# State update of a chunked scan as three half-precision products, with the decay spread moved to ScalarE

## Chip, cores and metric

One core of one Trainium2 chip runs the whole program in one launch. The metric is device microseconds from start to end of that launch.

## The reference, cut to what matters

The program is four layers, each an attention-like part and a feed-forward part. The change is in the attention part of layer 2, which is a selective state space scan. Cut to its core, with 64 heads of 64 channels, 128 state rows and 8 groups of 8 heads:

```python
proj = hidden @ in_proj_w.T           # gate, x, B, C, dt
xBC = silu(causal_conv(proj, 4 taps)) # x, B, C
dA, dtx = exp(dt_p * A), dt_p * x
state = state * dA_t + dtx_t * B_t    # one step per token, for each head
y_t = state @ C_t
out = (rmsnorm(y + x * D) * silu(gate)) @ out_proj_w.T
```

## The kernel before, in words

The scan is done in chunks of 128 tokens. There are 16 chunks of tokens (two sequences of eight) and 8 groups of heads, so the part makes 128 turns: an outer loop over groups `gi` (the first and the last written out, the six between in a hardware loop), and inside it `x` from 0 to 3 and `c` from 0 to 3, turn `j = 4x + c`. Below, "turn 12" is j = 12 of a group, and a "c=2 turn" is any of turns 2, 6, 10, 14.

Each engine has its order written out by hand, as a function `slot(gi, x, c)`, and the engines meet at semaphores.

**PE** in turn j: `chunk(j)` (L2482: the product of the old state with C, L2487; the products inside the chunk, eight heads, L2495; the state update, L2499), `along(j+1)` (L2460: eight 128x128 products, L2467, that carry the decay along the tokens), a tile of the input projection for the next four turns (`in_proj`, 12 matmuls of 128x512 f16 through the helper `three`, L257 to L259), `to_tokens(j+1)` (L2471: transposes, L2478 and L2480, that wait for the state on VectorE by `m4_sk`), a second tile, `out_proj(j-1)` (L2501: the sum of squares, L2507, then 12 matmuls), `between(j+2)` (L2449, L2456) and `b_dot_c(j+2)` (L2439, L2447). Only in c=0 and c=1 turns a third tile of the projection stands between `b_dot_c(j+2)` and `chunk(j+1)`. In c=2 and c=3 turns `chunk(j+1)` follows at once.

**VectorE** in turn j: `from_state` (L2225), `mask` (L2201), `state(j)` (L2228: L2237 scales the state in SBUF, L2238 adds PSUM), `outputs` (L2245, L2248), `stepped(j+1)` (L2210, two L2217: token inputs times the step, f32 into `m4_x12`), the taps of the convolution (L2181), `variance(j-1)` (L2254), `masked(j+1)` (L2208), more taps, and `add_out(j-1)` (L2257, L2266), which waits for the root from GpSimd (`m4_rk`). The pieces of the next weights (L1869) are made in turns 0, 1 and 10 to 13, the parameters of the next group (L2162, L2163) at the start of turn 12.

**ScalarE** in turn j: evictions of projection tiles (`before`, L2001 and L2002; `gate`, L2009), `step_decay(j+1)` (L2032, waits for `along`), `b_tokens(j+1)` (L2039), `skipped(j+1)` (L2047), `square(j)` (L2054), the nonlinearity of the convolution (L2018), `gated(j)` (L2060, waits for PE's `out_proj(j-1)`), and `decays(j+2)` (two L2026, behind a load of the table for Exp). Pieces of the weights are L1855 and L1858.

**GpSimd** in turn j: `spread(j+2)` (L2275: two L2282, 128x1024 f16, and two L2287, 128x512 f16, the heads' decays spread over channels into `m4_ab`, for `along`), the gating product (L2307), two sums of squares (L2309, waits for `square`; L2311), the low plane of the output (L2314), and `root(j-1)` (L2292, L2296).

A semaphore count stands behind each of these; a buffer is single unless said, so `m4_ab` is written again only when `along` has read it.

## Time and profile before

| | us |
|---|---|
| median of 3 runs | 4071.8 (4069.22 to 4078.91) |
| the profiled execution's own time | 4070.89 |
| span of its instructions | 4069.1 |
| first L2487 to last L2499 of the scan, on PE | 1478.8 to 3400.7 |
| PE busy | 3592.1 |
| VectorE busy | 2897.5 |
| ScalarE busy | 2361.3 |
| GpSimd busy | 2064.2 |

The profile is one execution. In a row of the timeline stand the start in us from the start of the span, the length in us, the engine and line, what is written and read, the shape and the count of instructions merged in that row; the bracket tells how long the engine was idle ahead of it and what ended the idle time. Matmuls overlap in the rows: the ends are modelled, so the distance from start to start is what one costs.

### The profile page before, as it was taken

How to read it: one execution, taken by the hardware profiler on the slowest of the kernel's cores; microseconds unless marked ns; L12 is line 12 of the kernel's file. 1: busy time of each engine (PE TensorE's matmuls, PEld its weight loads, DVE VectorE, ACT ScalarE, POOL GpSimd, SP SyncE). 2: the span in 40 equal slices, each digit the busy share in tenths (PEclk: the TensorE clock that was granted, in tenths of full speed). 3: DMA queues.
4: the chain of work that ended last, by engine and by line, in shares of the span. 5: the costliest groups of instructions: out<-in, count | busy, mean ns of one | idle time of the engine just before them, and what ended most of it. 6: DMA issues, size and time to landing. Idle time of an engine off the chain costs nothing.

```text
span 4069.1 us, 62802 instructions
## 1 busy us (share of the span) xinstructions
PE 3592.1 (88%) x21250; PEld 1808.2 (44%) x21250; DVE 2897.5 (71%) x4627; ACT 2361.3 (58%) x4071; POOL 2064.2 (51%) x1695
## 2 busy tenths in 40 slices
PE   3899998889888779999998999999999995776799
PEld 1344443323222335555555555555555553343344
DVE  4444337765764468888888898888888885657787
ACT  4533324555555466676676676676676663455665
POOL 4600000000000348777777877778777775546754
PEclk9999998998888899999999999999999997889999
DMA  3200011010100100000000000000000001012000
GB/s 105 68 6 1 1 25 24 1 19 9 29 9 2 41 13 1 25 13 23 16 7 25 8 26 14 15 24 1 26 13 21 11 1 65 1 52 76 13 11 32
DMA packets 58879, 88.92 MB, mean 22 GB/s; under 512 B 11429, under 2 KB 32440, under 8 KB 58548
## 3 DMA queue, kind: packets, MB, share of 16 engines
q1 hardware_dynamic: 57880, 84.15, 7.2%
q8 instruction: 183, 3.00, 0.3%
q14 instruction: 144, 1.18, 0.1%
q10 hardware_dynamic: 672, 0.59, 0.1%
HBM read 71.05 MB, written 6.85 MB: 19 GB/s over the span
## 4 chain that ended last, share of the span: by engine, by line
PE 62%; DVE 13%; issue 8%; ACT 6%; POOL 4%; SPq 0%; DVEq 0%; ACTq 0%; DMA 0%; POOLq 0%
PE psum L257 12%; PE psum L259 12%; PE psum L258 12%; PE psum L1392 3%; DVE arena L1554 2%; PE psum L2499 2%; PE psum L2487 2%; PE psum L1365 2%; PE psum L2495 2%; PE psum L2456 2%; PE psum L1376 2%; PE psum L3152 1%; PE psum L3153 1%; PE psum L2478 1%; DVE x L2181 1%
## 5 line engine op out<-in xcount | busy, mean ns | idle before, releaser
L257 PE MATMUL psum<-xt_hi,arena 128*128 128x512 f16 (+1 forms) x1920 | 740.8, 386 | 20.6 <-ACT arena L2009 5.9
L258 PE MATMUL psum<-xt_lo,arena 128*128 128x512 f16 (+1 forms) x1920 | 739.1, 385 | 0.0
L259 PE MATMUL psum<-xt_hi,arena 128*128 128x512 f16 (+1 forms) x1920 | 738.1, 384 | 0.0
L2282 POOL TENSOR_TENSOR arena<-arena 128x1024 f16<-128x1024 f16 x256 | 514.7, 2030 | 49.5 <-DVE arena L2093 32.4
L1554 DVE TENSOR_REDUCE arena<-psum 128x1 f32<-128x512 f32 (+3 forms) x608 | 371.1, 656 | 148.0 <-PE psum L1365 146.6
L257 PE MATMUL psum<-arena 128*128 128x512 f16 (+1 forms) x1152 | 418.9, 367 | 56.8 <-DVE arena L2917 25.5
L1505 ACT ACTIVATE arena<-psum 128x512 f32<-128x512 f32 x576 | 317.8, 598 | 254.0 <-PE psum L1376 180.8
L258 PE MATMUL psum<-arena 128*128 128x512 f16 (+1 forms) x1152 | 418.8, 367 | 0.0
L259 PE MATMUL psum<-arena 128*128 128x512 f16 (+1 forms) x1152 | 418.5, 367 | 0.0
L1310 POOL TENSOR_TENSOR rs<-sd,epsc 128x1 f32<-128x1 f32 x15 | 8.1, 541 | 791.5 <-DVE sd L1602 791.5
L2287 POOL TENSOR_TENSOR arena<-arena 128x512 f16<-128x512 f16 x256 | 315.0, 1249 | 4.6 <-PE psum L2467 4.6
L259 PEld LDWEIGHTS psum<-xt_hi,arena 128*128 128x128 f16 (+1 forms) x1920 | 190.3, 99 | 234.5 <-issue 13.9
L2181 DVE SCALAR_TENSOR_TENSOR x<-arena,x 128x512 f32<-128x512 f32 x288 | 285.4, 991 | 9.9 <-ACT x L2002 3.1
L257 PEld LDWEIGHTS psum<-xt_hi,arena 128*128 128x128 f16 (+1 forms) x1920 | 190.2, 99 | 226.1 <-issue 16.0
L2181 DVE SCALAR_TENSOR_TENSOR arena<-arena 128x512 f32<-128x512 f32 x288 | 276.3, 960 | 6.8
L2309 POOL TENSOR_TENSOR arena<-arena 128x256 f32<-128x256 f32 x128 | 147.3, 1151 | 253.5 <-ACT arena L2054 253.5
L258 PEld LDWEIGHTS psum<-xt_lo,arena 128*128 128x128 f16 (+1 forms) x1920 | 190.4, 99 | 191.9 <-issue 12.1
L1365 PE MATMUL psum<-arena 50*128 50x512 f16 (+3 forms) x768 | 200.1, 361 | 24.8 <-DVE arena L1554 23.5
L2001 ACT ACTIVATE arena<-psum 128x512 f32<-128x512 f32 x192 | 115.1, 600 | 170.6 <-PE psum L259 157.5
L257 PEld LDWEIGHTS psum<-arena 128*128 128x128 f16 x1152 | 124.6, 108 | 174.7 <-DVE arena L2917 28.6
L1376 PE MATMUL psum<-arena 51*128 51x512 f16 x576 | 193.2, 414 | 7.0 <-ACT arena L1505 4.2
L2032 ACT ACTIVATE arena<-psum 128x512 f32<-128x512 f32 x128 | 76.7, 599 | 201.0 <-PE psum L2467 201.0
(363 smaller groups left out, 8326.6 us busy)
## 6 DMA issues: line engine op xcount, KB each, us to landing
arena<-m_wi SPq DMA_DIRECT2D x64, 320.0 KB, 2.9
arena<-m_wo SPq DMA_DIRECT2D x32, 256.0 KB, 2.6
arena<-arena SPq DMA_DIRECT2D x90, 64.0 KB
x<-L_attn_x SPq DMA_DIRECT2D x4, 1024.0 KB, 5.2
arena<-gate_wT SPq DMA_DIRECT2D x16, 224.0 KB, 2.5
arena<-up_wT SPq DMA_DIRECT2D x16, 224.0 KB, 2.5
arena<-down_wT SPq DMA_DIRECT2D x14, 256.0 KB, 2.6
out<-x SPq DMA_DIRECT2D x3, 1024.0 KB, 4.3
```

What stands on the lines that cost most here:

```text
L257: nc.tensor.matmul(out, lh, rh, start=start, stop=False)
L258: nc.tensor.matmul(out, lh, rl, start=False, stop=False)
L259: return nc.tensor.matmul(out, ll, rh, start=False, stop=stop)
L1365: last = nc.tensor.matmul(out[:, a * w:(a + 1) * w], a2_qs[rows, h0 % (H2 // 2) + a, t * P:(t + 1) * P], a2_ks[b][rows, c:c + w], start=no ...
L1376: last = nc.tensor.matmul(out, a2_ks[b][rows, k * P:(k + 1) * P], a2_qs[rows, h4 // 2 * 4:h4 // 2 * 4 + 4, t * P:(t + 1) * P], start=True, ...
L1392: last = nc.tensor.matmul(psum[j * VW:(j + 1) * VW, 6, :], a2_v[b][:, g % (t + 1), :], a2_ps[(group2[p] + g) % 3][:, j, :], start=False, s ...
L1505: nc.scalar.activation(a2_ps[group % 3][:, u[0] % 4, :], psum[:, 3 + e % 3, :], ACT.Exp).then_inc(a2_e, 1)
L1554: nc.vector.tensor_reduce(a2_mx[:, q % 2, c // 512, h0:h0 + heads], bank[:, 0:heads * w].rearrange("p (h c) -> p h c", h=heads), AXX, ALU. ...
L2181: v = nc.vector.scalar_tensor_tensor(out=out, in0=m4_hb[:, i, j:j + GW], scalar=m4_cp[:, i * KC + j:i * KC + j + 1], in1=out, op0=ALU.mult ...
L2282: nc.gpsimd.tensor_tensor(m4_ar[:, q], heads[q].broadcast_to([P, HG, P]), m4_le.unsqueeze(1).broadcast_to([P, HG, P]), ALU.mult).then_inc( ...
L2287: nc.gpsimd.tensor_tensor(m4_ab[:, q].rearrange("p (h c) -> p h c", c=PS), heads[q].broadcast_to([P, HG, PS]), m4_on[:, 0:PS].unsqueeze(1) ...
L2309: nc.gpsimd.tensor_tensor(m4_sq[:, 0:2, :], m4_sq[:, 0:2, :], m4_sq[:, 2:4, :], ALU.add).then_inc(m4_qs, 1)
```

## The change

The input of the state update is split into a high and a low f16 plane on both sides, and the f32 product becomes three f16 products. ScalarE makes the high planes (`m4_bh` beside `m4_bt`, and `m4_x2h` in `stepped_high`, behind `square`), GpSimd the low ones (`b_low` behind the gating product, `stepped_low` behind the two sums of squares and ahead of L2314). So that f16 keeps its range, the step factor is multiplied by 16 and the result divided by 16 in the update of the state. The spread of the decays over the channels goes from GpSimd to ScalarE (`by_channel`, two Copy activations of 128x512 f16 behind `decays(j+2)`). Some semaphores are merged (`m4_cpk`, `m4_nwk`, `m4_dpk` into `m4_prk`, `z7_open` into `w7_o`), with the same points of waiting.

```diff
+        X2S = 16.0
@@ act_l2_attn
+            act.wait_ge(m4_tv, 4 + 3)
+            by_channel(act, 0, 0)
             decays(act, 0, 0)
             step_decay(act, 0, 0)
             b_tokens(act, 0, 0)
+            stepped_high(act, 0, 0)
+            by_channel(act, 0, 1)
...
                 square(act, gi, j)
+                if exists(gi, j + 1):
+                    stepped_high(act, *chunk_of(gi, j + 1))
...
                 if exists(gi, j + 2):
                     decays(act, *chunk_of(gi, j + 2))
+                    by_channel(act, *chunk_of(gi, j + 2))
@@ b_tokens
-            nc.scalar.activation(m4_bt, psum[:, 3, 0:P], ACT.Copy).then_inc(m4_bk, 1)
+            nc.scalar.activation(m4_bt, psum[:, 3, 0:P], ACT.Copy)
+            nc.scalar.activation(m4_bh, psum[:, 3, 0:P], ACT.Copy).then_inc(m4_bk, 1)
+
+        def stepped_high(act, gi, j):
+            n = gi * CG + j
+            act.wait_ge(m4_x2, n * 2 + 2)
+            act.wait_ge(m4_sn, n + 1)
+            nc.scalar.activation(m4_x2h, m4_x12[:, GF:], ACT.Copy).then_inc(m4_x2hi, 1)
+
+        def by_channel(act, gi, j):
+            n = gi * CG + j
+            act.wait_ge(m4_sp, n * 3 + 2)
+            for q, a in enumerate((m4_ah, m4_al)):
+                heads = a[:, ds(gi * HG + j * HS, HG)].unsqueeze(2)
+                v = nc.scalar.activation(m4_ab[:, q].rearrange("p (h c) -> p h c", c=PS), heads.broadcast_to([P, HG, PS]),
+                                         ACT.Copy)
+            v.then_inc(m4_abk, 1)
@@ dve_l2_attn, state
-                nc.vector.tensor_tensor(m4_dt2[:, hc], m4_dtp[:, hc], m4_v, ALU.mult).then_inc(m4_tv, 1)
+                nc.vector.scalar_tensor_tensor(out=m4_dt2[:, hc], in0=m4_dtp[:, hc], scalar=X2S, in1=m4_v,
+                                               op0=ALU.mult, op1=ALU.mult).then_inc(m4_tv, 1)
...
-            nc.vector.tensor_tensor(m4_st, m4_st, psum[:, 6, :], ALU.add).then_inc(m4_sk, 1)
+            nc.vector.scalar_tensor_tensor(out=m4_st, in0=psum[:, 6, :], scalar=1.0 / X2S, in1=m4_st, op0=ALU.mult,
+                                           op1=ALU.add).then_inc(m4_sk, 1)
@@ pool_l2_attn
-                pool.wait_ge(m4_sp, n * 3 + 2)
-                alone(pool)
-                for q in range(2):
-                    nc.gpsimd.tensor_tensor(m4_ab[:, q].rearrange("p (h c) -> p h c", c=PS),
-                                            heads[q].broadcast_to([P, HG, PS]),
-                                            m4_on[:, 0:PS].unsqueeze(1).broadcast_to([P, HG, PS]),
-                                            ALU.mult).then_inc(m4_ak, 1)
+            def b_low(gi, j):
+                n = gi * CG + j
+                pool.wait_ge(m4_bk, n + 2)
+                pool.wait_ge(m4_sn, n + 1)
+                nc.gpsimd.tensor_tensor(m4_bl, m4_bt, m4_bh, ALU.subtract)
+
+            def stepped_low(gi, j):
+                n = gi * CG + j
+                pool.wait_ge(m4_x2hi, n + 1)
+                nc.gpsimd.tensor_tensor(m4_x2l, m4_x12[:, GF:], m4_x2h, ALU.subtract).then_inc(m4_x2lo, 1)
...
                 nc.gpsimd.tensor_tensor(sg, m4_xc[x % 2][:, 2:6, tok], sg, ALU.mult).then_inc(m4_yn, 1)
+                if exists(gi, j + 1):
+                    b_low(*chunk_of(gi, j + 1))
...
                 nc.gpsimd.tensor_tensor(m4_sq[:, 0, :], m4_sq[:, 0, :], m4_sq[:, 1, :], ALU.add).then_inc(m4_qs, 1)
+                if exists(gi, j + 1):
+                    stepped_low(*chunk_of(gi, j + 1))
@@ pe_l2_attn
         def along(pe, gi, j):
-            pe.wait_ge(m4_ak, n * 4 + 4)
+            pe.wait_ge(m4_abk, n + 1)
...
-            pe.wait_ge(m4_x2, n * 2 + 2)
-            nc.tensor.matmul(psum[:, 6, :], m4_bt, m4_x12[:, GF:], start=True, stop=True).then_inc(m4_sn, 1)
+            pe.wait_ge(m4_x2lo, n + 1)
+            three(pe, psum[:, 6, :], m4_bh, m4_bl, m4_x2h, m4_x2l, True, True).then_inc(m4_sn, 1)
```

## Rows read from the trace of the kernel before

**Rows 1.** The page's busy times of the engines over the whole span.
```profile
PE 3592.1 (88%) x21250; PEld 1808.2 (44%) x21250; DVE 2897.5 (71%) x4627; ACT 2361.3 (58%) x4071; POOL 2064.2 (51%) x1695
```
**Rows 2.** Busy time by stretch: the whole scan, and four ordinary turns.
```profile
1478.00:3413.00 1935.00, 1836.69 (x11262) 1036.16 (x11261) 1630.28 (x2095) 1313.89 (x2299) 1501.70 (x1145) 0.99 0.05 16
2028.08:2085.68 57.60, 57.41 (x358) 32.72 (x357) 47.34 (x62) 40.12 (x71) 47.08 (x37) 1.00 0.00 1
```
**Rows 3.** Timeline of PE: a state update and what follows; two f16 matmuls.
```profile
2061.20 1.13 PE L2499 MATMUL psum<-tmp,arena 128*128 128x512 f32 x2
2062.16 0.61 PE L2467 MATMUL psum<-arena 128*128 128x128 f16 x8
...
2203.50 0.38 PE L258 MATMUL psum<-xt_lo,arena 128*128 128x512 f16 x1
2203.71 0.38 PE L259 MATMUL psum<-xt_hi,arena 128*128 128x512 f16 x1
```
**Rows 4.** Timeline, end of a c=2 turn (6): PE, then ScalarE.
```profile
2074.48 1.13 PE L2499 MATMUL psum<-tmp,arena 128*128 128x512 f32 x2
2075.44 0.61 PE L2467 MATMUL psum<-arena 128*128 128x128 f16 x8
...
2056.09 1.15 ACT L2018 ACTIVATE x<-x 128x512 f32<-128x512 f32 x2
2071.64 0.63 ACT L2060 ACTIVATE arena<-arena 128x512 f16<-128x512 f32 x1 [0.63 <-PE psum L259]
2073.59 1.09 ACT L2026 ACTIVATE xn<-psum 128x512 f32<-128x512 f32 x2
```
**Rows 5.** Groups of instructions by line and form, GpSimd (busy us, mean ns, idle before).
```profile
L2287 POOL TENSOR_TENSOR arena<-arena 128x512 f16<-128x512 f16 x256 | 315.0, 1249 | 4.6 <-PE psum L2467 4.6
L2309 POOL TENSOR_TENSOR arena<-arena 128x256 f32<-128x256 f32 x128 | 147.3, 1151 | 253.5 <-ACT arena L2054 253.5
L2314 POOL TENSOR_TENSOR arena<-x,arena 128x512 f16<-128x512 f32 x64 | 90.3, 1411 | 40.7 <-ACT arena L2060 40.7
```
**Rows 6.** Timeline, turns 0 and 1: GpSimd, VectorE, PE.
```profile
2225.36 1.34 POOL L2314 TENSOR_TENSOR arena<-x,arena 128x512 f16<-128x512 f32 x1 [0.22 <-ACT arena L2060]
...
2215.56 1.30 DVE L2237 TENSOR_TENSOR arena<-arena 128x512 f32<-128x512 f32 x1
2227.69 0.75 DVE L2266 SCALAR_TENSOR_TENSOR arena<-psum,arena 128x512 f32<-128x512 f32 x1 [0.44 <-POOL arena L2296]
...
2234.60 0.66 PE L2478 MATMUL psum<-ident,x 128*128 128x128 f32 x4 [1.20 <-DVE arena L2238]
2239.04 0.39 PE L257 MATMUL psum<-arena 128*128 128x512 f16 x1 [0.97 <-DVE arena L1869]
```
**Rows 7.** Timeline, end of turn 10 and turn 11: ScalarE, PE.
```profile
2132.34 1.09 ACT L2026 ACTIVATE xn<-psum 128x512 f32<-128x512 f32 x2
...
2133.28 0.61 PE L2467 MATMUL psum<-arena 128*128 128x128 f16 x8
2137.24 0.63 PE L2478 MATMUL psum<-ident,arena 128*128 128x128 f32 x4 [0.76 <-DVE arena L2238]
```
**Rows 8.** Timeline, turn 12: GpSimd, VectorE, PE.
```profile
2150.36 2.04 POOL L2287 TENSOR_TENSOR arena<-arena 128x512 f16<-128x512 f16 x2
...
2146.72 0.75 DVE L2266 SCALAR_TENSOR_TENSOR arena<-psum,arena 128x512 f32<-128x512 f32 x1 [1.98 <-POOL arena L2296]
2151.43 1.52 DVE L2237 TENSOR_TENSOR arena<-arena 128x512 f32<-128x512 f32 x1
...
2153.72 0.66 PE L2478 MATMUL psum<-ident,arena 128*128 128x128 f32 x4 [3.33 <-DVE arena L2238]
```
**Rows 9.** L2237 over the whole span: duration in ns, least, median, most.
```profile
L2237 DVE TENSOR_TENSOR arena<-arena x112: 682/1303/2097, 1482.4 to 3393.4; 128x512 f32<-128x512 f32 x112
```
**Rows 10.** PE's clock: a wait of PE, and a stretch after a later one (clock 0.50).
```profile
1666.30 0.66 PE L2478 MATMUL psum<-ident,arena 128*128 128x128 f32 x4 [2.35 <-DVE arena L2238]
...
2884.00:2888.00 4.00, 4.00 (x13) 2.01 (x13) 3.06 (x6) 2.69 (x7) 1.28 (x1) 0.50 0.02 4
```

More of the change, by code:

```diff
@@ L695, in build @@
         m4_ab = carve(117832, [2, GF], F16)
+        m4_x2h = carve(137376, [GF], F16)
+        m4_x2l = carve(138400, [GF], F16)
+        m4_bh = carve(136864, [P], F16)
+        m4_bl = carve(137120, [P], F16)
+        X2S = 16.0
         m4_e1 = carve(119880, [HG, P], F32)
@@ L734, in build @@
         m4_pi = sem("m4_pi")
-        m4_cpk = sem("m4_cpk")
-        m4_nwk = sem("m4_nwk")
+        m4_prk = sem("m4_prk")
         m4_whi = sem("m4_whi")
@@ L751, in build @@
         m4_xd = sem("m4_xd")
-        m4_dpk = sem("m4_dpk")
         m4_bk = sem("m4_bk")
         m4_x2 = sem("m4_x2")
+        m4_x2hi = sem("m4_x2hi")
+        m4_x2lo = sem("m4_x2lo")
+        m4_abk = sem("m4_abk")
         m4_ii = sem("m4_ii")
@@ L826, in build @@
         q7_done = sem("q7_done")
-        z7_open = sem("z7_open")
         z7_moved = sem("z7_moved")
@@ L1832, in group @@
                 if not is_last(gi):
-                    sp.wait_ge(m4_nwk, gi + 1)
+                    sp.wait_ge(m4_prk, gi * 3 + 3)
                     sp.dma_start(m4_pn.unsqueeze(1), A["m4_par"][:, ds(gi + 1, 1), :]).then_inc(m4_pi, 16)
@@ L1967, in slot @@
                 if x == 0 and c == 0:
-                    act.wait_ge(m4_nwk, gi + 1)
+                    act.wait_ge(m4_prk, gi * 3 + 3)
                     act.wait_ge(m4_op, gi * CG + 1)
@@ L1996, in before @@
                 act.wait_ge(m4_cy, gi * HF + (x + 1))
-                act.wait_ge(m4_cpk, gi + 1)
+                act.wait_ge(m4_prk, gi * 3 + 1)
                 if not is_first(gi, x * 4 - 4):
@@ L2043, in skipped @@
             if j == 0:
-                act.wait_ge(m4_dpk, gi + 1)
+                act.wait_ge(m4_prk, gi * 3 + 2)
             xs = m4_xc[j // 4 % 2]
@@ L2163, in conv_params @@
             nc.vector.tensor_scalar(m4_t3, m4_pn[:, 0:CT * KC].rearrange("p (i k) -> p i k", k=KC)[:, :, KC - 1], 1.0 / WS,
-                                    None, ALU.mult).then_inc(m4_cpk, 1)
-            dve.wait_ge(m4_cpk, gi + 1)
+                                    None, ALU.mult).then_inc(m4_prk, 1)
+            dve.wait_ge(m4_prk, gi * 3 + 1)
         def late_params(dve, gi):
-            nc.vector.tensor_scalar(m4_nw, m4_pn[:, CT * (KC + 1) + 4:], WS, None, ALU.mult).then_inc(m4_nwk, 1)
-            dve.wait_ge(m4_nwk, gi + 1)
+            nc.vector.tensor_scalar(m4_nw, m4_pn[:, CT * (KC + 1) + 4:], WS, None, ALU.mult).then_inc(m4_prk, 1)
+            dve.wait_ge(m4_prk, gi * 3 + 3)
         def skip_params(dve, gi):
@@ L2174, in skip_params @@
             nc.vector.tensor_scalar(m4_dp4, m4_pn[:, CT * (KC + 1):CT * (KC + 1) + 4], 1.0, None,
-                                    ALU.mult).then_inc(m4_dpk, 1)
+                                    ALU.mult).then_inc(m4_prk, 1)
         def convolve(dve, ch, gi, x, i):
@@ L2319, in pool_l2_attn @@
             spread(0, 1)
+            b_low(0, 0)
+            stepped_low(0, 0)
             def group(gi):
@@ L2451, in between @@
             n = gi * CG + j
-            pe.wait_ge(m4_ak, n * 4 + 2)
+            pe.wait_ge(m4_ak, n * 2 + 2)
             for q in range(2):
@@ L2763, in act_late @@
                 elif what == "w_open":
-                    act.wait_ge(w7_o, u + 1)
+                    act.wait_ge(w7_o, 2 + u + 1)
                     if u >= 2:
@@ L3039, in sp_zeros7 @@
             sp.dma_start(sh7, A["shifts"]).then_inc(z7_moved, 16)
-            sp.wait_ge(z7_open, 2)
+            sp.wait_ge(w7_o, 2)
             sp.dma_start(zeros7_gu, zf7[0:2 * KT].bitcast(F32)).then_inc(z7_moved, 16)
@@ L3051, in dve_zeros7 @@
                 nc.vector.tensor_scalar(zf7[a:b, 0:8 * w], zu7[a:b, 0:w, :].rearrange("p a b -> p (a b)"), 1.0, scale, ALU.add,
-                                        ALU.mult).then_inc(z7_open, 1)
+                                        ALU.mult).then_inc(w7_o, 1)
         def loads7(i):
```

## The prediction

> **What bounds the kernel now.** I read the page's busy times first, to see that PE is the busiest engine (88%) and that no other is above 71% [rows 1]. That is a mean over stages, so next I read busy time by stretch. In the scan PE is busy 1836.69 of 1935 us at a granted clock of 0.99, and in four ordinary turns 57.41 of 57.60 [rows 2]: there PE never waits, and whatever PE is spared or made to wait shows in the time at once. I call this the PE-bound case. The timeline then gives the turns where PE does wait, each a repeat of one pattern in all six groups of the loop: turns 0 and 1, where VectorE brings the state late and then a piece of weights [rows 6]; turns 11 and 12, also for the state [rows 7, 8]. Turns 13 to 15 run at VectorE's pace too, with small waits of PE. So some ten of sixteen turns are PE-bound, and six go by chains through VectorE, GpSimd and ScalarE.
>
> **The state product itself.** Before, from the start of L2499 to the start of the next matmul, is 2062.16 - 2061.20 = 0.96 us. An f16 matmul of the same 128x512 costs 2203.71 - 2203.50 = 0.21 to 0.22 from start to start [rows 3], three cost 0.65. The change spares 0.31 us a turn, and 128 turns would give 40 us if nothing else moved. As bounds: the second f32 record of L2499 is modelled to end later than the next start, so 0.31 is firm within 0.05.
>
> **The spread on ScalarE.** It adds two Copy activations of 512 elements behind `decays(j+2)`. Two neighbours of that size take 1.15 us together [rows 4] and start some 0.1 before the pair ahead of them has drained, so they add about 1.05 to 1.15. Nobody waited for the spread before, for GpSimd had it ready early. Now PE's `along` waits for it. In a c=2 or c=3 turn ScalarE's own chain starts when PE's `out_proj` ends: the gated copy at 2071.64, the table load, the decays from 2073.59 to 2074.68, then the copies to about 2075.75. PE's `along` started at 2075.44 and would now come at 2075.13 [rows 4]. PE waits 0.65, and the turn is 0.34 longer instead of 0.31 shorter. Both chains start at the same `out_proj`, so this doesn't slide away over turns. In c=0 and c=1 turns a third tile of some 2.6 us stands between, and nothing waits. Over four ordinary turns: 2 x -0.31 + 2 x 0.34 = +0.06. The whole gain is eaten in the stretch where it would have counted.
>
> **The high and low planes.** ScalarE gets one more copy (0.62) behind `square` and one of 128 elements (some 0.2, as a pipelined second) behind L2039. GpSimd loses two L2287 (1.25 each, 2.5 a turn) and gets `stepped_low`, which has the form of L2314, 1.1 to 1.7 in the timeline with a mean of 1.41 in the form shown, and `b_low`, a quarter of that size, 0.4 to 0.8 [rows 5]. `b_low` goes at nothing: behind the gating product GpSimd waits 253.5 us in 128 turns, 2 us each, for `square` [rows 5]; were that gone it would cost 0.6 us of a chain. `stepped_low` stands ahead of L2314 and of the root, and the root ends a wait of VectorE. In c=0 and c=1 turns of the ordinary kind VectorE then waits for PE's product anyway, so this costs nothing there. PE itself waits for `stepped_low` at the state product. In a c=2 turn it should end near 2073.9 to 2074.2, against L2499 at 2074.48: 0.3 us of room, and a miss below 0.65 hides in the wait for `along`. I take 0, with 0.3 a turn as the upper bound. The scaled add in place of L2238 costs 0.06 more, like L2266 (0.75) beside it.
>
> **One group, turn by turn.** PE-bound turns 2, 5, 6, 9: 4 x -0.31 = -1.24. Turns 3, 4, 7, 8, behind the missing third tile: 4 x 0.34 = +1.36. In turn 3 the root is 1.1 late and VectorE has little room: +0.3. Turns 10 and 11: the decays run 2132.34 to 2133.43, the copies to 2134.55, and `along` leaves at 2134.6 and not 2133.28; the old wait of 0.76 takes part of it [rows 7]: +0.55 for both. Turn 12: the chain is GpSimd's sums, L2314, root, L2266 [rows 8]. Without L2287 the gating product starts earlier, but the sums then wait for `square`, and with `stepped_low` the root comes some 0.4 later; against that, L2237 took 1.52 beside L2287 (2150.36 to 2152.40) and 0.68 at its fastest [rows 8, 9], so -0.8: -0.4. The extra copy behind L2039 delays the pieces of weights, on which the end of turns 12 and 1 hangs: +0.2 each. Turn 13: -0.1. Turns 14 and 15, at VectorE's pace: -0.35, the wait of the copies hidden behind VectorE's. Turn 0: root 0.3 later, absorbed by the loop's edge, L2237 1.30 to 0.68: -0.6. Turn 1: L2314 started 0.22 after its input, so `stepped_low` delays the root and L2266 (2227.69) nearly in full, and L2478 with them [rows 6]: +1.0. Sum: -1.24 + 1.36 + 0.3 + 0.55 - 0.4 + 0.4 - 0.1 - 0.35 - 0.6 + 1.0 = +0.9 a group, +6 over seven groups' worth.
>
> The page "SBUF — State Buffer" of the Trainium skill (section Who interferes with whom) says that a VectorE instruction with two SBUF inputs and a GpSimd one that reads SBUF take turns, each for a whole instruction; by it both 0.6 to 0.8 gains of L2237 are certain, and `stepped_low` beside L2208 would give up to one of its own durations back. The minimum in rows 9 agrees with the first half; no row here shows the second.
>
> **The clock.** PE's wait in turn 1 grows from 1.20 to about 1.2 + 1.0 + 0.31 = 2.5 us. PE waits up to 1.7 us in the scan left no slow matmuls behind; behind the one of 2.35 eight ran slow, and behind one of 3.35 the granted clock was 0.50 for some 5 us (that is 1.2 in place of 2.4 GHz) [rows 10]. Eight slow matmuls cost 1.7, of which the next wait (0.97 for a piece [rows 6]) takes part. At half the groups: +0.5 a group, +4.
>
> **The edges.** At the start ScalarE does the first spread ahead of the first decays, with PE waiting: +1.2, and the planes +0.8. In the last four turns GpSimd's chain is the bound, and loses 2.5 for 1.3 to 2 a turn: -2. Together 0.
>
> **The sum.** +6 + 4 + 0 = +10 on the profiled execution's 4070.9, which is 0.9 under the median of 4071.8 and the same for this purpose: 4081. A measurement here can tell about 0.3%, or 12 us, from no change.
>
> **Rivals.**
> *The copies hide (0.23).* If the two copies on ScalarE take less than 1.05 (a spread from 8 heads reads few elements), or ScalarE gets to the gated copy earlier, PE's `along` doesn't wait and 0.31 a turn stays in ten turns, with the relief of GpSimd on top: -3 to -5 a group, 4030 to 4055. For it: the decays of c=0 and c=1 turns are early. Against: every activation of 512 elements in the trace takes 0.58 or more, whatever it reads.
> *The root comes late and pulls the clock down (0.27), the rival on the slower side.* The place is `stepped_low` ahead of L2314 and the root; it decides from the point where VectorE's L2266 starts later than PE's product ends (0.9 us of room in c=1 turns, 0.3 in c=2 turns). At 1.7 us, the most that L2314 takes, it adds 0.4 to turns 1, 3, 7 and 12, and the wait of turn 1 crosses 2.35 in every group, which costs 1.7 more: some +3 a group more than forecast, 4100 to 4110.
> *PE waits for the low plane itself (0.08).* A `stepped_low` of 1.7 in c=2 turns misses PE by 0.3 beyond what `along` hides: 4 x 0.3 x 8 = +10, 4091.
> *The forecast (0.42):* 4066 to 4096 with its own error of 2 us a group.
>
> **How the numbers follow.** The likeliest case gives 4081. The range takes the forecast, the last rival, most of the slower one and the lower one down to 4043: 4043 to 4108. Faster than 4059: 0.24. Within 12 us: 0.36. Slower: 0.40, the slower rivals and the upper part of the forecast's own range.
>
> **What would show it.** Right: L257 to L259 in place of L2499 with 0.65 to the next matmul; L2467 idle ahead by 0.5 to 0.8 <-ACT in turns 3, 4, 7, 8; from L2487 to L2487 the ordinary c=1 and c=2 turns shorter by 0.31, the c=3 and c=0 turns longer by 0.34; L2478 in turn 1 waiting 2 to 2.6 for VectorE; L2237 at 0.7 in turns 0 and 12. Wrong: copies under 0.5 each and no wait ahead of L2467; PE idle ahead of the first of the three products, <-POOL; or an ordinary four turns away from 57.6 by more than 0.5.

## The result, and the profile after

The changed kernel takes 4089.32 us (median of six runs, 4086.58 to 4092.41) against 4071.12 for the kernel before in the same series: a ratio of 1.0048, with an interval of 1.0035 to 1.0062. It is slower by half a per cent. The forecast was 4081.0, its range 4043 to 4108, and "slower" had the largest of the three chances, 0.40. The profiled execution took 4086.58 us with a span of 4084.7.

The page's busy times, to be read against [rows 1]:

```profile
PE 3566.7 (87%) x21378; PEld 1791.8 (44%) x21378; DVE 2838.8 (69%) x4627; ACT 2575.0 (63%) x4583; POOL 1977.4 (48%) x1695
```

Every engine but ScalarE has less to do than before: PE 25 us less, VectorE 59, GpSimd 87; ScalarE has 214 more, and stays far from being the busiest. The time went up all the same, so the loss is in waits. By stretch (us, then busy time of PE, PE's weight loads, VectorE, ScalarE, GpSimd, then the granted clock): the whole scan, and the four ordinary turns 4 to 7, as in [rows 2].

```profile
1475.20:3413.20 1938.00, 1804.39 (x11337) 1015.34 (x11336) 1568.19 (x2084) 1525.39 (x2807) 1411.23 (x1136) 0.99 0.05 16
2032.59:2090.64 58.05, 56.53 (x362) 32.12 (x361) 45.78 (x62) 46.81 (x87) 43.27 (x37) 1.00 0.01 1
```

The four ordinary turns take 58.05 us where they took 57.60, with PE busy 56.53: PE, which never waited there, now waits. The timeline of PE and of ScalarE at the start of turn 4 shows for what.

```profile
2035.05 0.38 PE L259 MATMUL psum<-arena 128*128 128x512 f16 x1
2035.95 0.62 PE L2507 MATMUL psum<-arena 128*128 128x128 f16 x8 [0.53 <-ACT arena L2065]
```
```profile
2031.77 0.63 ACT L2088 ACTIVATE arena<-x 128x512 f16<-128x512 f32 x1 [1.15 <-PE psum L259]
2032.41 1.28 ACT L2038 ACT_TABLE_LOAD   x1
2033.71 1.09 ACT L2038 ACTIVATE arena<-psum 128x512 f32<-128x512 f32 x2
2034.68 1.15 ACT L2065 ACTIVATE arena<-arena 128x512 f16 x2
```

ScalarE starts the gated copy when `out_proj` ends (2031.77), then come the table load, the two decays and the two copies of the spread (L2065), done at 2035.83. PE's `along` (L2507) could have started at 2035.05 + 0.22 = 2035.27 and starts at 2035.95: 0.68 late. The row's own figure is 0.53, since the modelled end of the matmul ahead covers the rest.

The second half of the loss is in turns 1, 11 and 12. Turn 1, PE's rows that waited (in [rows 6] the same wait was 1.20), then turns 10 to 12 of VectorE and GpSimd:

```profile
1995.09 0.66 PE L2518 MATMUL psum<-ident,x 128*128 128x128 f32 x4 [1.91 <-DVE arena L2267]
1999.68 0.39 PE L257 MATMUL psum<-arena 128*128 128x512 f16 x1 [1.12 <-DVE arena L1874]
```
```profile
2134.76 2.11 DVE L2237 TENSOR_TENSOR arena<-arena 128x1024 f32<-128x1024 f32 x1
2136.79 4.73 DVE L2210 SCALAR_TENSOR_TENSOR arena<-arena 128x512 f32<-128x512 f32 x3
...
2154.40 0.75 DVE L2296 SCALAR_TENSOR_TENSOR arena<-psum,arena 128x512 f32<-128x512 f32 x1 [3.90 <-POOL arena L2330]
2155.06 1.20 DVE L2191 TENSOR_SCALAR arena<-arena 128x30 f32<-128x30 f32 x1
2156.18 1.93 DVE L2192 TENSOR_SCALAR m_t<-arena 128x6 f32<-128x6 f32 x1
```
```profile
2134.18 1.60 POOL L2324 TENSOR_TENSOR arena<-tmp,arena 128x512 f16<-128x512 f32 x1
2136.09 1.79 POOL L2352 TENSOR_TENSOR arena<-x,arena 128x512 f16<-128x512 f32 x1 [0.31 <-ACT arena L2088]
2137.84 0.99 POOL L2330 TENSOR_TENSOR arena<-arena,epsc 128x1 f32<-128x1 f32 x1
2138.81 4.47 POOL L2312 TENSOR_TENSOR arena<-arena 128x1024 f16<-128x1024 f16 x2
...
2153.81 0.55 POOL L2330 TENSOR_TENSOR arena<-arena,epsc 128x1 f32<-128x1 f32 x1
2154.33 3.75 POOL L2312 TENSOR_TENSOR arena<-arena 128x1024 f16<-128x1024 f16 x2
```

The same stretch of the kernel before, at the end of its turn 10:

```profile
2129.84 1.21 DVE L2208 TENSOR_TENSOR arena<-arena 128x1024 f32<-128x1024 f32 x1
2130.97 3.10 DVE L2181 SCALAR_TENSOR_TENSOR arena<-arena 128x512 f32<-128x512 f32 x3
```

The lines have moved: L2237 of the changed kernel is the masked decays (L2208 before), and the scaling of the state, L2237 before, is L2266 now. The masked decays start 0.6 us after GpSimd's new `stepped_low` (L2324). They took 1.21 and take 2.11: `stepped_low` ends at 2135.78, and 1.1 later, at 2136.87, they end. That is what they would take had they waited for the rest of the GpSimd instruction. The delay pushes the last three taps (L2210) further into the low half of the output, the root and the spread, and they take 4.73 for 3.10. VectorE comes to the state 2.5 us later in the turn for it (0.9 from the masked decays, 1.6 from the taps), and PE waits for that, 1.98 where it waited 0.76 [rows 7].

The lengths of the turns, from one start of the product with the state (L2487 before, L2527 after) to the next, means over the six groups of the loop, worked out from the timelines. The columns beside before and after are of experiments told below: "f32" is the spread on ScalarE with the one f32 product, "early" the spread moved ahead, "root" the root moved ahead, "both" the two together.

```
turn  before  after    f32  early   root   both
   0   16.81  16.51  16.26  16.43  15.64  15.65
   1   18.14  19.46  18.02  19.65  17.81  17.12
   2   13.27  12.97  13.27  12.97  12.97  12.97
   3   13.22  13.70  13.62  13.77  13.62  13.30
   4   15.55  15.95  15.95  15.24  15.95  15.24
   5   15.54  15.24  15.54  15.24  15.56  15.24
   6   13.27  12.97  13.27  12.97  12.97  12.97
   7   13.22  13.90  13.62  12.91  13.90  13.09
   8   15.55  15.95  15.95  15.24  15.95  15.24
   9   15.54  15.24  15.54  15.24  15.63  15.24
  10   13.54  13.40  13.54  13.33  13.40  13.33
  11   13.90  17.28  14.53  15.56  14.68  14.87
  12   20.49  19.16  17.04  19.44  17.21  16.15
  13   16.69  16.50  16.97  16.39  16.50  16.15
  14   13.61  12.97  13.60  13.67  12.97  12.99
  15   15.69  14.91  14.69  15.14  14.57  15.28
```

A group of sixteen turns takes 2.1 us more after the change, and the first group, which stands ahead of the loop, 5.3; from the first turn to the last the scan has grown from 1919.3 to 1938.0. The rest of the kernel moved by 3 us in all.

Where VectorE waits for the root, over the whole span, and what `stepped_low` takes (busy us, mean ns, idle before):

```profile
L2296 DVE SCALAR_TENSOR_TENSOR arena<-psum,arena 128x512 f32<-128x512 f32 x113 | 84.7, 750 | 203.7 <-POOL arena L2330 198.3
L2324 POOL TENSOR_TENSOR arena<-tmp,arena 128x512 f16<-128x512 f32 x128 | 197.8, 1546 | 1.5 <-ACT arena L2058 1.5
```

In the kernel before the same group (L2266) waits 134.6 us. These figures gave two theories to test. **S (the spread)**: the copies on ScalarE eat the gain of the product in the PE-bound turns. **R (the root)**: the low plane on GpSimd delays the root, and with it VectorE and the state, in turns 1, 11 and 12. "Theory A" in the expectations of experiments 1 to 4 is S and R together.

### The profile page after: what moved, and what is told of

Same layout as the page of the kernel before. It is cut to its first block, busy times and chain, and to the rows that moved or that the text cites. A ratio compares the mean times of both kernels' runs of the same rounds, so it can differ in the third digit from the quotient of the medians.

```text
span 4084.7 us, 63903 instructions
## 1 busy us (share of the span) xinstructions
PE 3566.7 (87%) x21378; PEld 1791.8 (44%) x21378; DVE 2838.8 (69%) x4627; ACT 2575.0 (63%) x4583; POOL 1977.4 (48%) x1695
## 3 DMA queue, kind: packets, MB, share of 16 engines
q14 instruction: 151, 1.24, 0.1%
## 4 chain that ended last, share of the span: by engine, by line
PE 51%; issue 12%; DVE 11%; POOL 10%; ACT 7%; SPq 0%; ACTq 0%; POOLq 0%; DVEq 0%; DMA 0%
PE psum L257 11%; PE psum L259 11%; PE psum L258 11%; PE psum L1397 3%; POOL arena L2312 3%; DVE arena L1559 2%; PE psum L1370 2%; PE psum L1381 2%; PE psum L3192 1%; PE psum L3193 1%; POOL arena L2345 1%; POOL arena L2352 1%; PE psum L1366 1%; PE psum L2535 1%; PE psum L2507 1%
## 5 line engine op out<-in xcount | busy, mean ns | idle before, releaser
L2312 POOL TENSOR_TENSOR arena<-arena 128x1024 f16<-128x1024 f16 x256 | 531.3, 2095 | 52.4 <-DVE arena L2121 32.5
L257 PE MATMUL psum<-arena 128*128 128x512 f16 (+1 forms) x1280 | 468.8, 370 | 58.2 <-DVE arena L2957 25.5
L1510 ACT ACTIVATE arena<-psum 128x512 f32<-128x512 f32 x576 | 317.8, 599 | 250.3 <-PE psum L1381 175.8
L258 PE MATMUL psum<-arena 128*128 128x512 f16 (+1 forms) x1280 | 467.3, 368 | 0.0
L259 PE MATMUL psum<-arena 128*128 128x512 f16 (+1 forms) x1280 | 467.1, 368 | 0.0
L2210 DVE SCALAR_TENSOR_TENSOR arena<-arena 128x512 f32<-128x512 f32 x288 | 297.6, 1033 | 6.8
L2210 DVE SCALAR_TENSOR_TENSOR x<-arena,x 128x512 f32<-128x512 f32 x288 | 286.9, 996 | 11.0 <-ACT x L2014 4.2
L2296 DVE SCALAR_TENSOR_TENSOR arena<-psum,arena 128x512 f32<-128x512 f32 x113 | 84.7, 750 | 203.7 <-POOL arena L2330 198.3
L257 PEld LDWEIGHTS psum<-arena 128*128 128x128 f16 x1280 | 136.9, 107 | 197.9 <-issue 41.7
L2013 ACT ACTIVATE arena<-psum 128x512 f32<-128x512 f32 x192 | 114.6, 597 | 158.9 <-PE psum L259 158.9
L2324 POOL TENSOR_TENSOR arena<-tmp,arena 128x512 f16<-128x512 f32 x128 | 197.8, 1546 | 1.5 <-ACT arena L2058 1.5
```

The source lines that it names most:

```text
L257: nc.tensor.matmul(out, lh, rh, start=start, stop=False)
L258: nc.tensor.matmul(out, lh, rl, start=False, stop=False)
L259: return nc.tensor.matmul(out, ll, rh, start=False, stop=stop)
L1510: nc.scalar.activation(a2_ps[group % 3][:, u[0] % 4, :], psum[:, 3 + e % 3, :], ACT.Exp).then_inc(a2_e, 1)
L2210: v = nc.vector.scalar_tensor_tensor(out=out, in0=m4_hb[:, i, j:j + GW], scalar=m4_cp[:, i * KC + j:i * KC + j + 1], in1=out, op0=ALU.mult ...
L2312: nc.gpsimd.tensor_tensor(m4_ar[:, q], heads[q].broadcast_to([P, HG, P]), m4_le.unsqueeze(1).broadcast_to([P, HG, P]), ALU.mult).then_inc( ...
```

## The experiments

Each has the kernel before on the same chip beside it; the ratio is to that kernel.

**1. The spread back on GpSimd.** It undoes the one part, on top of the planes.

```diff
+                pool.wait_ge(m4_sp, n * 3 + 2)
+                alone(pool)
+                for q in range(2):
+                    nc.gpsimd.tensor_tensor(m4_ab[:, q]..., heads[q].broadcast_to([P, HG, PS]),
+                                            m4_on[:, 0:PS].unsqueeze(1).broadcast_to([P, HG, PS]), ALU.mult)
...
-                    by_channel(act, *chunk_of(gi, j + 2))
```

> The changed kernel with the spread of the decays back on GpSimd (two L2287-like products a turn), the three f16 products and their planes kept. Theory A (two places cost time: the copies behind the decays on ScalarE make PE's along late in c=2 and c=3 turns, and the low plane ahead of the root makes VectorE late in turns 1, 3, 11, 12): no wait of PE for ScalarE ahead of along, turns 3, 4, 7, 8 at 12.9 and 15.2 us in place of 13.7 and 15.9, turns 1 and 11 as long as in the changed kernel or longer, 4065 (4050 to 4080). Rival B (GpSimd is then overfull, the spread was moved for that reason): all turns longer, above 4095.

Measured: 4163.92 us, ratio 1.0223 (1.0199 to 1.0246). PE no longer waits ahead of `along`, as S says, but the time is the rival's, though not quite by all turns: turn 2 is as long as in the changed kernel and turn 4 is 0.26 shorter. The page's busy times:

```profile
PE 3586.2 (86%) x21378; PEld 1806.0 (43%) x21378; DVE 2995.6 (72%) x4627; ACT 2447.0 (59%) x4327; POOL 2401.7 (58%) x1951
```

GpSimd is busy 424 us more than in the changed kernel, VectorE 157 more for the same 4627 instructions: they are stretched beside GpSimd's. PE then waits 0.7 to 3.3 us for the state in turns 0, 1, 3, 7, 8, 11, 12 and 15. In this order of GpSimd's work the planes can't be had without taking the spread off it; the root first with the spread on GpSimd was not tried.

**2. The spread on ScalarE, one f32 product.** It does the other part alone.

```diff
-            three(pe, psum[:, 6, :], m4_bh, m4_bl, m4_x2h, m4_x2l, True, True).then_inc(m4_sn, 1)
+            nc.tensor.matmul(psum[:, 6, :], m4_bt, m4_x12[:, GF:], start=True, stop=True).then_inc(m4_sn, 1)
...
-                if exists(gi, j + 1):
-                    stepped_high(act, *chunk_of(gi, j + 1))
...
-                    b_low(*chunk_of(gi, j + 1))
...
-                if exists(gi, j + 1):
-                    stepped_low(*chunk_of(gi, j + 1))
```

> The spread on ScalarE alone: the state product is one f32 product again, no planes. Theory A: turns 3, 4, 7, 8 about 0.34 longer than before (13.56 and 15.9), turns 0 and 12 shorter by 0.6 to 0.8 because L2237 no longer runs beside the spread on GpSimd, turns 1 and 11 as before: 4070 (4062 to 4078). Rival B (the load of ScalarE as such, not the place of the copies): PE waits for ScalarE in c=0 and c=1 turns too, above 4085.

Measured: 4056.32 us, ratio 0.996 (0.9943 to 0.9977), 14 us less than expected and below the expected range. The column "f32" of the table shows both sides. Turns 3, 4, 7 and 8 are 0.40 longer than before: S is right there. Turns 12 and 15 are 3.45 and 1.0 shorter. The spread alone was a gain, and the planes on top of it cost 1.0048 - 0.996 = 0.9%. VectorE in turn 12:

```profile
2157.59 1.20 DVE L2187 TENSOR_SCALAR arena<-arena 128x30 f32<-128x30 f32 x1
2158.70 0.16 DVE L2188 TENSOR_SCALAR m_t<-arena 128x6 f32<-128x6 f32 x1
```

The second of these scales six numbers of a row. It takes 0.16 in all six groups here, where it falls between two instructions of GpSimd and not beside one. In the changed kernel it takes 1.93 in all six. In the kernel before it takes 1.93 in five of them and 0.16 in group 3, as the rows of groups 2 and 3 show:

```profile
2148.50 1.93 DVE L2163 TENSOR_SCALAR m_t<-arena 128x6 f32<-128x6 f32 x1
...
2392.20 0.16 DVE L2163 TENSOR_SCALAR m_t<-arena 128x6 f32<-128x6 f32 x1
```

Both stand 4.28 us after the start of turn 12, both turns run at a granted clock of 1.00, and the turn takes 19.60 in group 2 and 17.96 in group 3. So whether this small instruction meets GpSimd's is worth 1.64 us of that turn.

**3. The spread earlier on ScalarE.** `by_channel(j+2)` is moved from behind the decays to ahead of the turn's second tile; nothing else.

```diff
+                if exists(gi, j + 2):
+                    by_channel(act, *chunk_of(gi, j + 2))
                 if nxt:
                     tile(act, *nxt, TILES[c][1])
                 square(act, gi, j)
...
                     decays(act, *chunk_of(gi, j + 2))
-                    by_channel(act, *chunk_of(gi, j + 2))
```

> The changed kernel with the two spread copies moved in ScalarE's order from behind the decays to ahead of the second projection tile of the turn. Theory A: the wait of PE ahead of along is gone, turns 3, 4, 7, 8, 12 lose 0.5 to 0.65 each, turns 1 and 11 stay: 4065 (4058 to 4075). Rival B (ScalarE's load): the wait moves to the gated copy or to the gates, and the time stays within 8 us of 4089.

Measured: 4067.38 us, ratio 1.0 (0.9988 to 1.0012), 0.5% or some 20 us below the changed kernel. PE's waits in the scan ahead of `along` and ahead of `to_tokens` (which waits for the state), first of the changed kernel, then of this one:

```profile
L2507 PE MATMUL psum<-arena 128*128 128x128 f16 x1008 | 77.8, 219 | 37.8 <-ACT arena L2065 37.2 <-ACT arena L2038 0.5
L2518 PE MATMUL psum<-ident,arena 128*128 128x128 f32 x252 | 40.2, 283 | 32.5 <-DVE arena L2267 31.8
L2518 PE MATMUL psum<-ident,x 128*128 128x128 f32 x252 | 39.5, 280 | 21.0 <-DVE arena L2267 18.3 <-DVE arena L2262 2.3
```
```profile
L2508 PE MATMUL psum<-arena 128*128 128x128 f16 x1016 | 77.7, 218 | 2.3 <-ACT xn L2039 1.3 <-ACT arena L2039 0.5 <-issue 0.4
L2519 PE MATMUL psum<-ident,arena 128*128 128x128 f32 x256 | 41.0, 284 | 46.1 <-DVE arena L2268 46.1
L2519 PE MATMUL psum<-ident,x 128*128 128x128 f32 x252 | 40.7, 286 | 32.7 <-DVE arena L2268 24.6 <-DVE arena L2263 7.8
```

The wait ahead of `along` is gone (37.8 to 2.3), but the one for the state has grown from 53.5 to 78.8. Where PE had stood for the spread, VectorE had caught up in its shadow: in turn 1 PE waited 0.51 for the copies and 1.91 for the state, and now waits 2.59 for the state. Turns 4, 7 and 8 fell by 0.7 to 1.0, so S is right there. Turn 3 did not fall, since PE now waits 0.92 for the state in it; turn 12 rose by 0.3, and turn 11, which was said to stay, fell by 1.7. Those go by VectorE and GpSimd.

**4. The low plane earlier on GpSimd.** `stepped_low` goes right behind `b_low`, ahead of the sums of squares, and `stepped_high` behind the skip products on ScalarE.

```diff
                     skipped(act, *chunk_of(gi, j + 1))
+                    stepped_high(act, *chunk_of(gi, j + 1))
...
                 square(act, gi, j)
-                if exists(gi, j + 1):
-                    stepped_high(act, *chunk_of(gi, j + 1))
...
                     b_low(*chunk_of(gi, j + 1))
+                    stepped_low(*chunk_of(gi, j + 1))
                 pool.wait_ge(m4_qk, n + 2)
...
-                if exists(gi, j + 1):
-                    stepped_low(*chunk_of(gi, j + 1))
```

> The changed kernel with the high plane made behind the skip scaling and the low plane ahead of the sums of squares on GpSimd, in its wait for the squares. Theory A: the root is on time again and the low plane no longer runs beside VectorE's second set of taps, so turn 1 loses 1.0, turn 11 up to 2.5, turn 3 0.3: 4065 (4055 to 4078). Rival C (the lateness of turn 11 is from ScalarE's load, not from GpSimd's order): turn 11 stays above 16.5 us, 4082 or more.

Measured: 4109.84 us, ratio 1.0092 (1.0073 to 1.0112), a miss by 45 us. Turn 11 did fall, to 14.53, but turns 1, 10, 13 and 15 rose by 1.0 to 1.6. The high plane was moved in the same run, so what follows is read from rows and was not taken apart by a run of its own. PE in turn 1:

```profile
2000.93 0.66 PE L2516 MATMUL psum<-ident,x 128*128 128x128 f32 x4 [1.70 <-DVE arena L2266]
2006.62 0.61 PE L257 MATMUL psum<-arena 128*128 128x512 f16 x1 [2.23 <-DVE arena L1874]
```

The second wait, for a piece of weights that VectorE scales, was 1.12. The low plane now runs beside VectorE's first taps (1987.10 to 1988.70, the taps 3.27) and the sums start only behind it. In the wait for the squares GpSimd is idle, but VectorE isn't: an idle place of GpSimd's is no free place.

**5 and 6. One f32 product, with the spread early; and with the root first as well.** The second moves the root from the end of GpSimd's turn to right behind the second sum, ahead of the low half of the gated output.

```diff
                 nc.gpsimd.tensor_tensor(m4_sq[:, 0, :], m4_sq[:, 0, :], m4_sq[:, 1, :], ALU.add).then_inc(m4_qs, 1)
+                if not is_first(gi, j - 1):
+                    root(*chunk_of(gi, j - 1))
...
                 nc.gpsimd.tensor_tensor(m4_yl, sg, m4_yh, ALU.subtract).then_inc(m4_ylo, 1)
-                if not is_first(gi, j - 1):
-                    root(*chunk_of(gi, j - 1))
```

> Spread on ScalarE ahead of the second tile, f32 state product, no planes. Theory A (place of the copies): the 0.23 us wait of PE ahead of along that the f32 version with late copies still shows in turns 3, 4, 7, 8, 11, 12, 15 is gone, so about 0.4 each in turns 3, 4, 7, 8 below e2: 4056 - 8 x 1.6 = 4043 (4038 to 4052). Rival B (the gain of e2 came from luck in turn 12, where two small VectorE operations slipped between GpSimd's): turn 12 back at 19 or more and the time at 4055 to 4065.

> As e5, and the root goes ahead of L2314 (the low plane of the output) on GpSimd, right behind the sums. If the root's lateness holds VectorE up in turns 1 and 12 (theory A): VectorE's wait for the root shrinks by 1.1 or more in each turn, turns 1 and 12 lose up to 1 each: 8 to 16 us below e5. Rival C (VectorE's lateness is contention with GpSimd, not the root's time): within 5 us of e5, or slower.

Measured: 4036.67 (ratio 0.9911, 0.9894 to 0.9928), and 4029.3 (0.9888, 0.9871 to 0.9904). Without the planes the early spread is worth 0.5%, as with them. Turn 12 is 16.4, not back at 19, so the rival of experiment 5 is out. The root's place brings another 0.2%, or 7 us, which is less than expected and hardly clear of the intervals, though VectorE's wait for the root fell from 178.6 to 62.8 us over the scan. Most of that wait cost nothing there: in both runs turn 11 is what is long, 16.4 and 16.5.

**7. The planes, the spread early and the root first.** Experiment 3 with the edit of the root, which here passes `stepped_low` too.

> The planes kept, the spread early (as e3), and the root ahead of the low plane of the steps on GpSimd. Theory A: turns 1, 3 and 12 lose the 1.0, 0.3 to 0.9 and 0.5 that the low plane put in front of the root; PE may wait 0.3 to 0.7 for the low plane in c=2 turns; 4050 (4042 to 4062). Rival C (contention of the low plane with VectorE's masked product and taps): turn 11 stays at 15.5 and the time within 8 us of e3, 4060 to 4072.

Measured: 3998.52 us (3995.5 to 4003.36), ratio 0.9819 (0.9803 to 0.9836). It is faster than both kernels: 1.8% under the kernel before, where the expected 4050 would have been 0.5%. VectorE's wait for the root over the scan, then PE's waits as above, then the ordinary turns 4 to 7:

```profile
L2297 DVE SCALAR_TENSOR_TENSOR arena<-psum,arena 128x512 f32<-128x512 f32 x113 | 84.5, 747 | 75.1 <-POOL arena L2331 70.3 <-PE psum L259 4.8
```
```profile
L2508 PE MATMUL psum<-arena 128*128 128x128 f16 x1016 | 78.4, 219 | 2.3 <-ACT xn L2039 1.3 <-issue 0.5 <-ACT arena L2039 0.5
L2519 PE MATMUL psum<-ident,arena 128*128 128x128 f32 x256 | 40.9, 283 | 16.0 <-DVE arena L2268 12.9
L2519 PE MATMUL psum<-ident,x 128*128 128x128 f32 x252 | 38.6, 276 | 7.8 <-DVE arena L2263 5.7 <-DVE arena L2268 1.8
```
```profile
2009.20:2065.74 56.54, 56.25 (x363) 32.35 (x362) 43.49 (x63) 46.66 (x87) 43.41 (x37) 1.00 0.01 1
```

The wait for the state is 23.8 us where it was 53.5 and 78.8, and the four ordinary turns take 56.54. Against 57.60 of before that is 1.06 less, most of the 1.24 that four times 0.31 makes. Beside experiment 6, which differs only in the product and its planes, it is 0.7% or some 28 us faster: once neither the spread nor the root stands in the way, the planes bring most of 128 x 0.31 = 40 us. A part of the whole gain is the clock: here the granted clock is 1.00 in every turn of the six groups, where experiment 3 shows less in turns 1, 11 and 12, the changed kernel too, and the kernel before in turn 12.

**8. No low plane.** Experiment 3 without making `stepped_low` in the turns; PE's three products stay and read a stale plane, so that term of the state product is left out of the computation in effect.

> As e3 (planes, spread early), but the low plane of the stepped inputs is made once at the start and not again, so that part of the state update is left out; the three products on PE stay. It shows what the subtraction on GpSimd costs in all. Theories A and C together: turn 1 falls to 18.2, 3 to 12.9, 11 to 14 or less, 12 to 18.5 or less: 4067 - 8 x (1.4 + 0.9 + 1.5 + 1) = 4030 (4022 to 4042). Rival: the planes' cost lies with ScalarE's extra copies, and the time stays above 4055.

Measured: 4032.2 us, ratio 0.9904 (0.9882 to 0.9926). The time is as expected: one instruction of 1.5 us a turn, on an engine that is busy for 48% of the span (and 73% of the scan), costs 1% where it stands ahead of the root. What it costs behind the root wasn't measured; experiment 7 has it there and is 34 us faster than this run, so the order of the two is worth more than leaving it out. But turn 11 was 17.40, and not 14 or less. Its VectorE and GpSimd rows:

```profile
2119.10 1.40 DVE L2238 TENSOR_TENSOR arena<-arena 128x1024 f32<-128x1024 f32 x1
2120.43 4.81 DVE L2211 SCALAR_TENSOR_TENSOR arena<-arena 128x512 f32<-128x512 f32 x3
```
```profile
2120.44 1.16 POOL L2351 TENSOR_TENSOR arena<-x,arena 128x512 f16<-128x512 f32 x1 [1.01 <-ACT arena L2089]
2121.56 1.00 POOL L2331 TENSOR_TENSOR arena<-arena,epsc 128x1 f32<-128x1 f32 x1
2122.53 4.47 POOL L2313 TENSOR_TENSOR arena<-arena 128x1024 f16<-128x1024 f16 x2
```

The taps take 4.81 here without a low plane: one of the three falls on the spread's first instruction of 2.2 us. Turn 11 isn't `stepped_low` alone, then, but whether the last taps are through when the spread starts. Experiments 5, 6 and 10 say the same: none has a low plane of the steps, and turn 11 takes 16.3 to 16.5 in each.

**9 and 10. The root first alone: on the changed kernel, and on the kernel before.** The same edit of the root, with the spread where each kernel has it.

> The changed kernel, with nothing but the root moved right behind the second sum of squares, ahead of the low plane and the low half of the gated output; the spread stays where the change put it. Theory A (both parts are separate gains: the spread is late for PE by 0.5 us in six to eight turns of 16, and the root is late for VectorE in turns 11, 12, 13): about 4089 - 69 = 4020 us, the 20 us that the early spread gave still missing. Rival B (the root only pays when PE's wait for the spread is gone): 4060 us or more. The wait of add_out for the root in microseconds 1478 to 3400 falls from 185 to below 90 by either.

> The kernel before, with nothing but the root moved right behind the second sum of squares, ahead of the low half of the gated output. Theory A (the root's lateness was a loss of the kernel before as well, 128 us of waits of VectorE in the loop, most of it in turns 11 to 13): 20 to 45 us faster than before, 4026 to 4050 us. Rival B (in the kernel before the root stood behind one GpSimd operation only, and what it waits behind then, the f16 products' GpSimd load, is a matter of the change): within 10 us of before.

Measured: 4042.95 us, ratio 0.9933 (0.9911 to 0.9956), and 4041.06, ratio 0.9912 (0.988 to 0.9944). The kernel before gains 0.9% by it, as its theory A had it: the order was a loss there too. It is not the root's wait alone, though: turn 12 falls by 3.85 with L2163 at 0.16 in every group, and turn 11 rises by 2.36, with its last taps beside the spread. The changed kernel gains 1.0048 - 0.9933 = 1.15%. The time lies between what its two theories said (4020, and 4060 or more): each edit is a gain by itself (the early spread 0.5%, the root 1.15%), and together they bring 2.3%, more than the sum, since either leaves PE in the other's wait. In experiment 3 the wait for the state grew to 78.8 us; in this one the wait ahead of `along` is 45.3, where the changed kernel has 37.8. VectorE waited 185.4 us for the root over the scan in the changed kernel and 55.8 in this one.

**11. The root ahead of both sums.** As experiment 7, with the root moved on, into GpSimd's wait for the squares.

> The early spread and the root of the turn before moved further, ahead of both sums, into GpSimd's wait for the squares. Theory A (the remaining waits are those of PE for the low plane, and the root's 0.9 us out of the line of sums and low plane brings that plane forward): 5 to 20 us below the kernel with the root behind the sums (3998.5), 3979 to 3994 us. Rival B (the variance comes late there, GpSimd stands and the sums are late for PE's sum of squares): 4010 us or more.

Measured: 4007.74 us, ratio 0.9837 (0.9808 to 0.9866). It isn't better than experiment 7 (0.9819), nor told apart from it, and both expectations missed, the one below and the one above. VectorE's wait for the root is all but gone (8.3 us), and its taps ran at full pace (2.75 for three, for 3.87 in experiment 7), but the low plane came late for PE in turn 11:

```profile
L2297 DVE SCALAR_TENSOR_TENSOR arena<-psum,arena 128x512 f32<-128x512 f32 x113 | 84.0, 744 | 40.4 <-PE psum L259 32.1 <-POOL arena L2331 8.3
```

In group 2 PE waits 2.39 us there for `stepped_low`, where it waits 0.40 for it and 1.38 for the state in experiment 7. Theory A had it that the low plane would come forward; in the same turn the root waits 5.06 us for the variance there and the sums stand behind it.

**12. A third copy.** The changed kernel with one more Copy between the two of the spread, to a place that nobody reads.

```diff
                 heads = a[:, ds(gi * HG + j * HS, HG)].unsqueeze(2)
+                if q:
+                    nc.scalar.activation(m4_cc.rearrange("p (h c) -> p h c", c=PS), heads.broadcast_to([P, HG, PS]), ACT.Copy)
                 v = nc.scalar.activation(m4_ab[:, q]..., heads.broadcast_to([P, HG, PS]), ACT.Copy)
```

> The changed kernel with a third Copy of the same shape between the two of the spread, into a place that nobody reads. If the two copies are what sets turns 3, 4, 7 and 8 (ScalarE's activations 0.52 us from start to start), each of these turns grows by 0.52 us over the changed kernel: 14.22, 16.47, 14.42 and 16.47 us; the turns that the copies don't reach (2, 6: 12.97) stay. Sum about 6 times 2.1 to 4 us and what turns 11, 12 and 15 add: 4102 to 4125 us. Rival: the wait of PE for the spread belongs to what stands ahead of the copies on ScalarE, and a third one hides in part: below 4098 us.

Measured: 4110.68 us, ratio 1.0088 (1.0058 to 1.0118). PE and ScalarE at the start of turn 4:

```profile
2056.72 0.45 PE L2511 MATMUL psum<-arena 128*128 128x128 f16 x5 [1.05 <-ACT arena L2069]
```
```profile
2054.92 0.63 ACT L2069 ACTIVATE arena<-arena 128x512 f16 x1
2055.44 0.63 ACT L2067 ACTIVATE arena<-arena 128x512 f16 x1
2055.96 0.63 ACT L2069 ACTIVATE arena<-arena 128x512 f16 x1
```

The wait grew from 0.53 to 1.05, by the 0.52 from start to start of one copy, and turns 3, 4 and 8 by 0.44, 0.51 and 0.52. Turn 7 grew by 0.24 only and turn 6, which was said to stay, by 0.50; why isn't shown. The copies set turns 3, 4 and 8, as S says.

## Why the prediction was right, and where it was not

The direction was right and the time within 8 us, well inside the range, but the forecast loss of 9 us is half of the 18 measured. Of its steps:

**The product, right.** Turns 2, 5, 6 and 9 are 0.30 shorter; forecast 0.31. **The spread in ordinary turns, right.** Forecast was a wait that starts 0.65 late and +0.34 for turns 3, 4, 7 and 8. It is 0.68, and +0.48, +0.40, +0.68, +0.40. Turns 4 to 7 together grew by 0.45 where 0.06 was forecast; what is above the forecast lies mostly in turn 7. Its wait is 0.81 and not 0.53, because the gated copy ahead of it starts 12.42 us into turn 6, where it starts 12.15 into turn 2; why it does isn't shown. Experiments 2, 3 and 12 show the cause by changing the product, the place and the count of the copies one at a time. The rival by which the copies hide fell with the wait ahead of L2507.

**Turn 1, right in cause, and a little short.** Forecast +1.2 with the extra copy; it is +1.32, with PE's wait for the state 1.20 before and 1.91 after, where 2 to 2.6 was forecast. Experiment 2, without the planes, has 18.02 there, so it is the planes. The wait is shorter than forecast because PE stands 0.51 for the copies ahead of it, which no step had in a c=1 turn; in experiment 3, without that, it is 2.59. The granted clock fell in two of the six groups, at 0.4 us each.

**The edges, wrong.** They were put at 0 together. The first group took 5.3 us more, 3.1 of it in turn 1, where PE waits 2.72 for the copies; the last group took 1.0 more, and the rest of the kernel 3 less.

**Turns 11 and 12, wrong in both terms.** The failing step is "Turns 10 and 11 ... +0.55 for both" and "Turn 12 ... -0.4". Turn 11 rose by 3.38, turn 12 fell by 1.33, turn 10 by 0.14; together +1.91, against +0.35 in the sum with the +0.2 for the extra copy. Two terms were mis-sized there.

GpSimd's relief from the spread was -3.45 in turn 12 and -1.0 in turn 15 (experiment 2 against before), where -0.8 stood. I priced only the scaling of the state (L2237 before), which did fall to 0.68 in turns 0 and 12. The 3.45 of turn 12 can be taken apart by its six groups before: four show a granted clock of 0.84 or 0.92 and take 20.8 to 21.9, one takes 19.6 at 1.00, and group 3 takes 17.96 with L2163 at 0.16. The clock is then 1.2 of the mean, L2163 in the shadow of the spread 1.4, and 0.9 is left, which fits what the root comes earlier in the turn (it ends 2.5 us after the start before, 1.6 in experiment 2).

Against that, the planes cost +2.75 in turn 11 and +2.12 in turn 12 (after against experiment 2), where some +0.4 stood: `stepped_low` was counted as a delay of the root, and not as an instruction that VectorE's masked decays have to wait out, nor as what moves the last taps onto the spread. Of the 2.75, 0.8 is the clock.

The two errors are 3.6 and 4.5 us a group and nearly cancel. The total was near by that luck; the row that shows what the spread's instructions do beside VectorE, L2163 at 1.93, stands in the trace of before, and no step of the prediction uses it. That row also sorts the runs: the small instruction takes 1.93 in the changed kernel and in experiments 1, 3, 4 and 12, which are all at 1.00 or above, and 0.16 in at least five of the six groups in experiments 2 and 5 to 11, which are all below. At 1.64 us a group that is some 10 us, an estimate, of what those runs gain; no run changed it alone.

The page "SBUF — State Buffer" of the Trainium skill (section Who interferes with whom) was quoted for its rule, with the remark that no row showed the half of it that a low plane beside the masked decays would pay for. The trace after agrees with it: the masked decays took 2.11 in place of 1.21 and ended 1.1 us after `stepped_low` did. Had the rule been carried into the sum of turns 10 and 11, it would have given +0.9 there, of the 3.38.

**The slower rival** had the right place, `stepped_low` ahead of the root, and by experiments 7 and 9 that place decides the sign of the whole change. It had the size wrong, since the clock, which made most of its price, did little in turn 1. Over a whole group the most that the clock can have taken, as the length of the turns times what the granted clock lacked of 1.00, is 1.7 us before and 2.3 after: 0.6 more. Turns 11 and 12 hold after what turn 12 held before, and turn 1 the 0.6, near the +0.5 of the forecast; but the next wait took most of it, and turn 1 is only 0.14 longer for it on the mean. Turns 14 and 15 fell by 1.42 where 0.35 was forecast; how much of it is the root in turn 14 and how much the spread isn't settled.

## What to carry to other kernels

Price a GpSimd instruction by what VectorE does beside it and by what stands behind it, not by GpSimd's own busy share: one of 1.5 us a turn cost 1% here ahead of the root, and a small VectorE instruction that takes twelve times its time is where to see it. When a change adds work to an in-order engine, look first at what another engine waits for behind it, and try the same order without the change as well: moving the root by one place gave the old kernel 0.9%, the new one with its spread moved too 2.3%, and turned the loss of the f16 products into a gain of 0.7%. Measured against the old kernel with the same edit (0.9912), the best version of the change (0.9819) is worth 0.9%, not 1.8%. A stall that sits in another's shadow comes out only when both are taken away, so edits that look worth little by themselves are to be tried together.
